# First step of a graph-network kernel: the subtraction that makes the low half of the encoded edge attributes goes from VectorE to GpSimd, ahead of each group's gathers

## The reference, cut to what matters

```python
edge_attr = swish(edge_attr_raw @ enc_W + enc_b)          # 50000 x 128, once
for _ in range(4):
    e_in = concatenate([edge_attr, x[src], x[dst]])
    e_upd = layernorm(swish(e_in @ eW1 + eb1) @ eW2 + eb2, eg, ebeta)
    edge_attr = edge_attr + e_upd
    agg = segment_sum(edge_attr, dst, 3125)
    n_in = concatenate([x, agg])
    x = x + layernorm(swish(n_in @ nW1 + nb1) @ nW2 + nb2, ng, nbeta)
return layernorm(x0 + x)
```

## Time and profile before

| what | us |
|---|---|
| median of 3 runs | 2530.68 (2520.82 to 2542.6) |
| the profiled execution, its own time | 2528.01 |
| span of the profiled execution | 2526.3 |
| first step's gathers, first to last issue | 71.57 to 644.49 |
| mean granted TensorE clock | 0.984 |

### The profile page before, as it was taken

The page is one execution under the profiler, slowest core; times in us unless marked ns, Lnnn a source line. Parts: engine busy times, 40 slices in busy tenths (PEclk is TensorE's granted clock), DMA queues, the critical chain, the costliest instruction groups (busy, mean ns, idle before and its releaser), DMA issues.

```text
span 2526.3 us, 82599 instructions
## 1 busy us (share of the span) xinstructions
PE 2357.6 (93%) x27988; PEld 1848.9 (73%) x27988; DVE 2216.7 (88%) x6127; ACT 1912.4 (76%) x5248; POOL 1623.0 (64%) x1588
## 2 busy tenths in 40 slices
PE   5799999999979999999988999999997999999995
PEld 2577777777747787888765787888874788878874
DVE  7699999999747999999965999999984899999997
ACT  3577777777548888888846888888864888888884
POOL 2677777777117777777505777777712777777750
PEclk9899999999989999999999999999998999999998
DMA  5666666666347888888626888888834666676640
GB/s 167 180 203 204 202 201 203 207 204 205 101 150 217 254 253 253 256 255 262 214 98 192 254 256 254 258 257 254 254 126 159 201 205 203 205 207 203 207 144 27
DMA packets 382921, 515.14 MB, mean 204 GB/s; under 512 B 58581, under 2 KB 256356, under 8 KB 382490
## 3 DMA queue, kind: packets, MB, share of 16 engines
q1 hardware_dynamic: 303572, 302.15, 37.3%
q0 software_dynamic: 75264, 205.62, 28.9%
q10 hardware_dynamic: 3654, 1.99, 0.3%
HBM read 390.48 MB, written 119.05 MB: 202 GB/s over the span
## 4 chain that ended last, share of the span: by engine, by line
PE 39%; POOL 26%; DVE 15%; issue 10%; DMA 7%; ACT 2%; DVEq 0%; ACTq 0%; SPq 0%; POOLq 0%
POOL arena L1646 26%; PE psum L1687 8%; PE psum L1714 7%; PE psum L1675 7%; DMA arena<-node_tables,idx_all 7%; DVE arena L1942 3%; PE psum L1745 3%; PE psum L2142 3%; PE psum L1667 3%; PE psum L1699 2%; PE psum L2181 2%; DVE arena L1962 2%; PE psum L2155 2%; DVE arena L1901 2%; PE psum L1709 1%
## 5 line engine op out<-in xcount | busy, mean ns | idle before, releaser
L1646 POOL DMA_INDIRECT arena<-node_tables,idx_all x1568 | 1609.8, 1027 | 812.0 <-issue 424.9
L1811 ACT ACTIVATE arena<-psum 128x1024 f16<-128x1024 f32 x392 | 401.1, 1023 | 399.3 <-PE psum L1687 399.3
L1901 DVE SCALAR_TENSOR_TENSOR arena<-psum,arena 128x1024 f16<-128x1024 f32 x392 | 478.0, 1219 | 156.8 <-PE psum L1714 89.0
L1714 PE MATMUL psum<-w_hi,arena 128*128 128x128 f16 x6272 | 589.4, 219 | 3.9 <-DVE arena L1901 3.9
L1714 PE MATMUL psum<-w_lo,arena 128*128 128x128 f16 x3136 | 545.6, 219 | 0.0
L1714 PEld LDWEIGHTS psum<-w_hi,arena 128*128 128x128 f16 x6272 | 498.2, 98 | 17.2 <-DVE arena L1901 5.5
L1687 PE MATMUL psum<-arena,w_hi 128*128 128x512 f16 x1568 | 470.4, 382 | 1.4 <-ACT arena L1848 1.3
L1675 PE MATMUL psum<-ident,arena 128*128 128x128 f16 x6272 | 418.6, 220 | 39.5 <-DMA arena<-node_tables,idx_all 38.2
L1675 PEld LDWEIGHTS psum<-ident,arena 128*128 128x128 f16 x6272 | 378.8, 98 | 69.9 <-DMA arena<-node_tables,idx_all 62.2
L1824 ACT ACTIVATE arena<-psum 128x128 f32<-128x128 f32 x1568 | 412.6, 290 | 5.5 <-PE psum L1714 5.5
L1812 ACT ACTIVATE psum<-psum 128x1024 f32<-128x1024 f32 x392 | 399.5, 1019 | 0.0
(11 more groups left out here) (177 smaller groups left out, 3130.1 us busy)
## 6 DMA issues: line engine op xcount, KB each, us to landing
state<-arena SPq DMA_DIRECT2D x294, 256.0 KB
arena<-state SPq DMA_DIRECT2D x294, 256.0 KB
arena<-node_tables SPq DMA_DIRECT2D x784, 64.0 KB
arena<-matrices SPq DMA_DIRECT2D x294, 128.0 KB
node_tables<-arena SPq DMA_DIRECT2D x100, 256.0 KB, 2.2
arena<-node_tables,idx_all POOLq DMA_INDIRECT x1568
arena<-rel_rows SPq DMA_DIRECT2D x98, 128.0 KB
matrices<-arena SPq DMA_DIRECT2D x98, 128.0 KB
```

The source lines that it names most:

```text
L1646: pool.indirect_dma_start(out=rows[n % R][:, t, :], out_offset=None, in_=p_table, in_offset=bass.IndirectOffsetOnAxis(ap=idx_all[:, n % G1 ...
L1714: x = pe.matmul(ps_v(k2)[:, t * P:(t + 1) * P], h[k2][:, half, t * P:(t + 1) * P], w[:, half, :], start=False, stop=half == 1 and h is hl, ...
L1811: act.activation(hh[k2], ps_h(k2), ACT.Silu).then_inc(S("hh"), 1)
L1901: dve.scalar_tensor_tensor(hl[k2], ps_h(k2), 1.0, hh[k2], ALU.mult, ALU.subtract).then_inc(S("hl"), 1)
```

## The change

The subtraction of the first step is taken out of VectorE's program and put into GpSimd's. Ahead of the gathers of groups 0 and 1 stands the subtraction of the same group; ahead of group 2 none; ahead of group `n` from 3 to 97 that of group `n-1`; behind the last gathers that of group 97. On GpSimd it is a `tensor_tensor` subtract of the same operands and shapes. Its wait for `hi` goes with it, and it counts the same `lo`. Nothing changes in steps two to four.

```diff
@@ first_matrices, begin_dve (VectorE) @@
-                def low(n):
-                    if n >= G1:
-                        return
-                    dve.wait_ge(Z("hi"), n + 1)
-                    dve.scalar_tensor_tensor(turned_in[n % RE][:, 1, :], e0f[n % 2], 1.0, turned_in[n % RE][:, 0, :],
-                                             ALU.mult, ALU.subtract).then_inc(Z("lo"), 1)
-
-                return matrices_of, low
+                return matrices_of
...
-                low(0)
@@ pool (GpSimd) @@
+                def first_low(n):
+                    pool.wait_ge(Z("hi"), n + 1)
+                    pool.tensor_tensor(turned_in[n % RE][:, 1, :], e0f[n % 2], turned_in[n % RE][:, 0, :],
+                                       ALU.subtract).then_inc(Z("lo"), 1)
+
                 for n in range(s * G1, (s + 1) * G1):
+                    if n < 2:
+                        first_low(n)
+                    elif 3 <= n < G1:
+                        first_low(n - 1)
                     if n >= R:
                         pool.wait_ge(S("src"), n - R + 1)
                     for t in range(TPG):
...
+                    if n == G1 - 1:
+                        first_low(n)
@@ slot (VectorE) @@
                     matrices_of(n + 2)
-                    first_low(n + 1)
                     low(n)
```

More of the change, by code:

```diff
@@ L1541, in matrices_of @@
                                       rel_all[:, :, n:n + 1].to_broadcast([P, TPG, P]), ALU.is_equal, saturate=False).then_inc(Z("oh"), 1)
-                def low(n):
-                    if n >= G1:
-                        return
-                    dve.wait_ge(Z("hi"), n + 1)
-                    dve.scalar_tensor_tensor(turned_in[n % RE][:, 1, :], e0f[n % 2], 1.0, turned_in[n % RE][:, 0, :],
-                                             ALU.mult, ALU.subtract).then_inc(Z("lo"), 1)
-                return matrices_of, low
+                return matrices_of
             def begin_dve(self, dve):
-                matrices_of, low = self.first_matrices(dve)
+                matrices_of = self.first_matrices(dve)
                 for k in range(R):
@@ L1990, in seed_chunk @@
                                              ALU.mult, ALU.add).then_inc(SU("seeded"), 1)
-                matrices_of, first_low = self.first_matrices(dve) if s == 0 else (nothing, nothing)
+                matrices_of = self.first_matrices(dve) if s == 0 else nothing
                 def slot(n):
```

## The result

| what | before | after |
|---|---|---|
| median of 6 runs each | 2530.89 (2520.82 to 2542.6) | 2566.61 (2552.3 to 2570.07) |
| ratio, with its 95% interval | | 1.0122 (1.0103 to 1.014) |
| the profiled execution: time, span | 2528.01, 2526.3 | 2552.34, 2550.6 |
| gathered matmuls of group 97 (TensorE) | 649.13 | 679.20 |

The change costs 1.2%, 36 us by the medians. The forecast was slower by 65 us: the direction is right and the time lies in the range, but the loss is about half of what was summed up. The sum was made against the profiled execution, and there it can be read directly: the first step ends 30.1 us later (679.20 - 649.13), not 65.

What follows compares the result with a forecast made beforehand. VectorE bounds the first step before, GpSimd after: 5.00 + 1.15 + 0.09 + 0.30 = 6.54 us a group over 98 groups, with end corrections +65 us on 2528.0, so 2593 us, range 2551 to 2651.

Steps and rivals of the forecast that it cites:

- GpSimd becomes the bound of the first step: First step: GpSimd's 6.24 us a group before any stretch exceeds VectorE's 5.29 and TensorE's 5.73.
- TensorE as the limit of any gain: First step: TensorE's matmuls stand 5.73 us a group apart, so even a free subtraction gains at most 16 us.
- The subtraction at 1.15 us: GpSimd, first step: each of 98 moved 128x512 subtractions takes 1.15 us, from a straight line through two other operations.
- the 5.00 + 0.09 + 0.30 around it: GpSimd, per group: 5.00 us for four unstretched gathers with gaps, 0.09 to the next instruction, 0.30 of stretch.
- the forecast's own band: First step: 6.3 to 6.9 us a group, +42 to +100 us, given a chance of 0.62.
- GpSimd loses little: Rival, first step: VectorE and GpSimd miss each other, subtraction costs 1.03; 6.12 us a group, +23 us, 2551; chance 0.16.
- The first rival: First step: GpSimd and VectorE hold each other, stretch stays 0.88; 7.12 us a group, +123 us, 2651; chance 0.12.
- VectorE's busy share down to 0.8: Sign in the first step: VectorE's busy share falls from 0.99 to about 0.8.
- TensorE waits for gathers in nearly every group: Sign in the first step: TensorE waits for gathers in nearly every group instead of 3 times.
- `hi` in time, no chain: First step: `hi` comes 1.9 to 4.2 us early; rival that its dependency loop bounds, +135 us with 8 us landings, chance 0.04.
- the clock at 1.00: First step: TensorE's new gaps cost nothing while its clock stays up; under 1.00 would show the forecast wrong.
- Nothing gives it back: After the first step: steps two to four and the node phase recover none of the +65 us.

Runs made afterwards that it cites:

- the fill: Changed kernel with a GpSimd memset of 1250 scratch columns in place of the subtraction, behind the same wait for `hi`; 2559.66 us, ratio 1.0106.
- no_low: Changed kernel without the first step's subtraction on either engine, the low halves zeroed once; 2518.01 us, 0.9927 of the kernel before.
- full_no_oh: Changed kernel without the first step's comparison L1539 on VectorE, its matrices staying zero; 2551.29 us, 1.0101 of the kernel before.
- again: The changed kernel, unaltered, run once more for a second profile; 2557.95 us.
- the split kernels: Changed kernel with the subtraction shared by GpSimd and VectorE: by halves of the columns (2554.15 us) or by odd and even groups (2552.42 us).
- late_full: Changed kernel with the subtraction of group m ahead of the gathers of m+2 instead of m+1; 2587.76 us, 1.0223 of the kernel before.

## Why the prediction was right in direction and twice too large

- **GpSimd becomes the bound of the first step: right.** It runs from 71.37 to 677.12 us without idle time but issue, and neither the fill (nearly the same loss) nor a relieved VectorE (no gain) changes that. TensorE as the limit of any gain, about 16 us: right, no_low ends 15 us under before with TensorE full, though at 5.82 us a group and not at 5.73.
- **The subtraction at 1.15 us: right,** 1.169 measured.
- **The term that failed: the 5.00 + 0.09 + 0.30 around it,** gathers with their gaps, the step to the next instruction and the stretch, 5.39 in the forecast's 6.54 us a group. Measured were 383.4 / 98 = 3.91 for the gathers and (105.4 + 2.3) / 98 = 1.10 for the gaps, 5.01 together. The stretch is 3.91 - 3.80 = 0.11, not 0.30. The gaps are 1.10, not 1.29: I counted 0.30 ahead of each of four gathers and a 0.09 on top, but the gather behind the subtraction has only 0.16 and the subtraction itself 0.01. The two errors of 0.19 each, less 0.02 for the subtraction, make 0.36 us a group; times 98 that is 35 us, and 65 - 35 = 30 is what the first step lost. By this the group fell outside the forecast's own band of 6.3 to 6.9 us (+42 to +100). The stretch was put at 0.30 because five instructions could be hit and one of them was long. The long one was not stretched at all (1.169 us on average, 1.17 in the undisturbed group); where it met VectorE, VectorE waited.
- **Nearest rival:** "GpSimd loses little" (6.12 a group, +23) against 6.18 and +30. It is the same mechanism with small terms, and its reason, a phase in which the two miss each other, is half of what the trace shows: the gathers mostly miss (22 of 392 over 1.1 us), while the subtraction meets a small VectorE instruction about 40 times in 86 groups, and that one does the waiting (L314, 591 ns on average). The first rival's point that both engines hold each other is there too; but what it set against itself, that VectorE has the slack to wait, holds.
- **VectorE's busy share down to 0.8: wrong,** 516.64 / 530 = 0.97. Its own work did fall, but the time for which it is held is shown as busy. full_no_oh shows that it doesn't set the pace nevertheless.
- **TensorE waits for gathers in nearly every group: wrong,** 18 times, 11.5 us. Its slack went to waits for the held VectorE as well (L1966, 21.8 us).
- **A reading in passing:** of the 109.7 us of idle time ahead of the gathers the forecast called almost all "issue"; that is 90.5, and 19.2 stand beside TensorE's name. Those gaps too are of 0.30 us (18.0 us in 59 waits), so that the sum of 5.00 a group doesn't change.
- **`hi` in time, no chain; the clock at 1.00: right.** One wait of 0.5 us, and PEclk 1.00 in the window.
- **"Nothing gives it back":** the 30.1 us at the end of the first step are 24.3 at the end of the span (2550.6 - 2526.3). The later steps vary by as much between two executions of the same kernel: the first gathers of steps two and three are 593.9 us apart in the profile after (771.09 and 1365.01) and 598.9 in again (769.54 and 1368.41); before they were 599.1.

What stays open: the six runs of the changed kernel lie at 2552.3 (two) and at 2566 to 2570 (four), and both of its profiles are of runs at 2552 and 2558. That leaves some 10 us between the difference of the profiled executions (24 us) and that of the medians (36 us) without a row. How the split kernels divide their 6.05 us between the two engines' holding is not settled either: only that taking L1539's 0.6 us from VectorE ends it, and that removing GpSimd's reads doesn't. Nor is it known what decides where the two programs meet, on which the stretch hangs (0.11 us a group here, 0.42 in late_full).

## What to carry to other kernels

Before work is moved to an engine that shows 80% busy, add the idle time that nothing explains: GpSimd's 0.30 us of issue ahead of each gather filled it already. What it could give back was its stretch, 5.89 - 5.00 = 0.89 us a group, and the subtraction with its gaps took 6.04 - 5.00 = 1.04. Price a moved instruction by the gaps on both its sides in a row of its own kind, not by a gap added once more. And test "which engine bounds" by relieving each in turn: a busy share that includes held time (0.97 on VectorE here) answers that wrongly. One such run isn't enough where order matters: without L1539 the changed kernel kept its time, and without the gains it became slower.

## What was not expected of the hardware

- A GpSimd arithmetic instruction starts 0.01 us behind a gather, and the gather behind it needs 0.16 of issue, where one behind a gather needs 0.30.
- Which engine pays for the sharing changed with the order: before, the gathers (1.170 us on average, now 0.978), after, VectorE's smallest instructions: one of 8 columns and 0.16 us lasts 1.66 beside a subtraction of 1.17, in some 40 of 86 groups.
- A fill on GpSimd, which reads nothing, doubles a one-operand VectorE instruction (L1538, 548 to 1109 ns) and leaves the two-operand ones alone (L1539 682, L316 174).
- With the work split between two engines, each put at about 5.6 us a group of its own and so under the 5.73 of the third, the group took 6.04 to 6.09 us. Both engines show held instructions; that these alone explain it is not shown.
